# Routing sums of a two-layer transformer kernel, moved to four column tiles of the matrix engine

## What is computed

```
x = x + L0_xattn(layernorm(x), ctx)      # 8 heads
x = x + L0_ffn(layernorm(x))             # 16 experts of 64, the best 4 by sigmoid score
x = x + L1_xattn(layernorm(x), ctx)      # top-32 attention, FiLM, a long convolution, an MLP
x = x + L1_ffn(layernorm(x))             # 8 experts, each picks its best 512 tokens
```

```
logits = layernorm(x) @ expert_sel.T          # 16 per token
probs  = sigmoid(logits); take the best 4; divide by their sum
out    = sum over experts of  prob * relu(layernorm(x) @ keys[e]) @ values[e]
```

## Time and profile before

| what | value |
|---|---|
| median of three runs | 1471.42 us (1470.21 to 1471.47) |
| span of the profiled execution | 1470.0 us |
| TensorE busy | 1280.7 us, 87% |
| VectorE busy | 925.6 us, 63% |
| ScalarE busy | 465.3 us, 32% |
| GpSimd busy | 325.8 us, 22% |
| first routing matmul of the eight batches | 103.6, 240.0, 362.8, 485.4, 607.8, 739.4, 865.6, 974.8 us |

### The profile page before, as it was taken

The page is one execution under the profiler, slowest core; times in us unless marked ns, Lnnn a source line. Parts: engine busy times, 40 slices in busy tenths (PEclk is TensorE's granted clock), DMA queues, the critical chain, the costliest instruction groups (busy, mean ns, idle before and its releaser), DMA issues. The chain is left out here.

```text
span 1470.0 us, 17444 instructions
## 1 busy us (share of the span) xinstructions
PE 1280.7 (87%) x5222; PEld 768.4 (52%) x5222; DVE 925.6 (63%) x3439; ACT 465.3 (32%) x837; POOL 325.8 (22%) x598
## 2 busy tenths in 40 slices
PE   4677968999999899899989989999887719999996
PEld 3444644465466455546545554645444516666764
DVE  6647789767767776865677786686987382211110
ACT  2544432042324315213431521343132433233221
POOL 3121221023112203201220320222102303332331
PEclk9677989999999999989999999999998858999999
DMA  9002000200300400030030003003000025453321
GB/s 293 9 15 59 18 1 22 51 18 15 88 18 1 102 18 1 25 79 18 1 102 17 1 16 87 16 2 87 7 1 1 30 93 173 109 145 87 90 37 18
DMA packets 44904, 72.51 MB, mean 49 GB/s; under 512 B 8101, under 2 KB 26760, under 8 KB 44682
## 3 DMA queue, kind: packets, MB, share of 16 engines
q1 hardware_dynamic: 38666, 62.87, 14.6%
q0 software_dynamic: 6144, 8.52, 3.3%
HBM read 58.27 MB, written 13.07 MB: 49 GB/s over the span
## 5 line engine op out<-in xcount | busy, mean ns | idle before, releaser
L773 POOL TENSOR_SCALAR ve<-mv 128x2 f32<-128x2 f32 x74 | 16.6, 225 | 552.9 <-DVE mv L1041 552.8
L1604 PE MATMUL ps<-x,keys 128*128 128x512 f32 x256 | 127.0, 620 | 0.5 <-DVE hT L1133 0.4
L1761 PE MATMUL ps<-hT,values 128*128 128x512 f32 x256 | 118.2, 592 | 0.0
L2189 PE MATMUL experts_ps<-experts_yT,experts_fc 128*128 128x512 f32 x256 | 111.9, 595 | 1.2 <-ACT experts_yT L2114 1.2
L2201 PE MATMUL experts_ps<-experts_fc,experts_hT 128*128 128x256 f32 x512 | 112.0, 379 | 0.8 <-ACT experts_hT L2126 0.8
L1604 PE MATMUL ps<-zT_second,w 128*128 128x512 f32 x224 | 102.3, 598 | 7.8 <-ACT big L1552 7.2
L2201 PEld LDWEIGHTS experts_ps<-experts_fc,experts_hT 128*128 128x128 f32 x512 | 96.6, 190 | 14.6 <-ACT experts_hT L2126 1.6
L1604 PE MATMUL ps<-w,big 128*128 128x256 f32 x448 | 98.9, 380 | 0.8 <-ACT big L1552 0.8
L2098 DVE SCALAR_TENSOR_TENSOR experts_o<-experts_ps,experts_wh,experts_b2w 128x256 f32<-128x256 f32 x32 | 15.5, 484 | 128.7 <-PE experts_ps L2201 128.7
L2126 ACT ACTIVATE experts_hT<-experts_ps,experts_b 128x512 f32<-128x512 f32 x64 | 44.0, 687 | 155.4 <-PE experts_ps L2189 155.4
L1604 PEld LDWEIGHTS ps<-w,big 128*128 128x128 f32 x448 | 84.3, 190 | 13.8 <-ACT big L1552 1.6
(11 more groups left out here) (435 smaller groups left out, 2489.7 us busy)
## 6 DMA issues: line engine op xcount, KB each, us to landing
gT<-expert_gates SPq DMA_DIRECT2D x16, 1024.0 KB, 9.6
experts_fc<-in_fc1T SPq DMA_DIRECT2D x8, 1024.0 KB, 5.2
experts_fc<-in_fc2T SPq DMA_DIRECT2D x8, 1024.0 KB, 8.7
xT<-in_xT SPq DMA_DIRECT2D x8, 512.0 KB, 3.5
x<-in_x SPq DMA_DIRECT2D x8, 512.0 KB, 3.5
expert_table<-tb SPq DMA_DIRECT2D x7, 528.0 KB, 7.6
out_x<-x SPq DMA_DIRECT2D x7, 512.0 KB, 6.9
w<-in_W SPq DMA_DIRECT2D x2, 1024.0 KB, 9.4
```

The lines of the kernel that those rows point to most:

```text
L773: nc.gpsimd.tensor_scalar(o, i, c, None, ALU.add).then_inc(*tick(*event))
L1604: last = nc.tensor.matmul(o, l, r_, start=start, stop=stop)
L1761: last = nc.tensor.matmul(bank("O2", k), S["values"][:, c, k * P:(k + 1) * P], hT[:, c % RING, :], start=(c == 0), stop=(c == HC - 1))
L2189: last = nc.tensor.matmul(g_bank(m), fc1[e % 3][:, k, m * P:(m + 1) * P], yT[e % 2][:, k, :], start=(k == 0), stop=(k == DC - 1))
```

## The change

Both sums are computed by halves of the tokens (256 columns each) on four column tiles: scores and mean of the first half at PSUM partitions 0 to 16 and of the second at 32 to 48, the square sums of the halves at partitions 64 and 96. All lie in the first 256 columns of the bank. The column of 1/256 moves from the end of `sel` to its start, so that in each tile the sum that gives a mean stands at the tile's first partition.

One copy takes 97 partitions x 256 columns, now into a part of `e_buf` (`logits`) in place of `lists`. Partitions between the tiles hold what the bank held before; they are copied and not used. Two transposes (97 partitions x 128 tokens each) replace four. A transpose now holds the tokens of tile `g` of both halves, so token tile `t = 2h + g`, and VectorE's two readers take their elements in that order with patterns of one dimension more.

```diff
-            loads["sel"] = wb("sel", [P, DC, E0 + 1])[:, :, 0:E0], ...
+            loads["sel"] = wb("sel", [P, DC, E0 + 1])[:, :, 1:E0 + 1], ...
-            blank(g.memset(S["sel"][:, :, E0:E0 + 1], 1.0 / D))
+            blank(g.memset(S["sel"][:, :, 0:1], 1.0 / D))
 ...
                 for k in range(DC):
-                    nc.tensor.matmul(o[64:64 + E0 + 1, :], S["sel"][:, k, :], xp[:, k, :], start=(k == 0), stop=(k == DC - 1))
+                    for h in HALVES:
+                        nc.tensor.matmul(o[32 * h:32 * h + E0 + 1, 0:2 * P], S["sel"][:, k, :], xp[:, k, h * 2 * P:(h + 1) * 2 * P],
+                                         start=(k == 0), stop=(k == DC - 1))
                 pe.wait_ge(*at(b, "sq", DC - 1))
                 for k in range(DC):
-                    last = nc.tensor.matmul(o[96:97, :], S["sel"][:, k, E0:E0 + 1], sq[:, k, :], start=(k == 0), stop=(k == DC - 1))
+                    for h in HALVES:
+                        last = nc.tensor.matmul(o[64 + 32 * h:65 + 32 * h, 0:2 * P], S["sel"][:, k, 0:1], sq[:, k, h * 2 * P:(h + 1) * 2 * P],
+                                                start=(k == 0), stop=(k == DC - 1))
 ...
-                evacuate(b, lists[route_rows, :], bank("LG")[route_rows, :], "LG")
+                evacuate(b, logits, bank("LG")[routed, 0:2 * P], "LG")
 ...
-                for t in range(NT):
-                    last = nc.tensor.transpose(bank("LT")[:, t * 33:(t + 1) * 33], lists[route_rows, t * P:(t + 1) * P], ident[route_rows, route_rows])
+                for g in range(2):
+                    last = nc.tensor.transpose(bank("LT")[:, g * routed.stop:(g + 1) * routed.stop], logits[:, g * P:(g + 1) * P], ident[routed, routed])
 ...
-                    nc.vector.tensor_copy(ms[:], lg[:, :, E0:2 * E0 + 1:E0]).then_inc(*tick("ms"))
+                    nc.vector.tensor_copy(ms[:].rearrange("p (h g) k -> p g k h", g=2),
+                                          lg[:, :, 0:routed.stop:32].rearrange("p g (k h) -> p g k h", k=2)).then_inc(*tick("ms"))
 ...
-                    nc.vector.tensor_tensor(sg[:, :, 0:E0], lg[:, :, 0:E0], rr[:].to_broadcast([P, NT, E0]),
+                    nc.vector.tensor_tensor(sg[:].rearrange("p (h g) e -> p h g e", g=2)[:, :, :, 0:E0],
+                                            lg.rearrange("p g (h e) -> p h g e", h=2)[:, :, :, 1:E0 + 1],
+                                            rr[:].rearrange("p (h g) o -> p h g o", g=2).to_broadcast([P, 2, 2, E0]),
                                             ALU.mult).then_inc(*tick("emptied", "LT"))
```

More of the change, by code:

```diff
@@ L437, in layers_block @@
         sq = e_buf
+        logits = e_buf[0:3 * 32 + 1, 0, 0:2 * P]
         mx, sm, rs = (sb(n, [P, NT, H0]) for n in ("mx", "sm", "rs"))
@@ L443, in layers_block @@
         g16 = lists[32:32 + E0, :]
-        route_rows = slice(64, 64 + 33)
+        routed = slice(0, 3 * 32 + 1)
         ms, v0, ve0, rr = sb("route_ms", [P, NT, 2]), sb("route_var", [P, NT, 1]), sb("route_ve", [P, NT, 1]), sb("route_rstd", [P, NT, 1])
@@ L540, in layers_block @@
         half = [slice(0, 512), slice(512, HID)]
-        to_centre = [(S["sel"], slice(0, E0)), (S["keys"], half[0]), (S["keys"], half[1]), (S["gate_w"], slice(0, E1)),
+        to_centre = [(S["sel"], slice(1, E0 + 1)), (S["keys"], half[0]), (S["keys"], half[1]), (S["gate_w"], slice(0, E1)),
                      (S["w1"], half[0]), (S["w1"], half[1])]
@@ L1081, in gates @@
                 if part == 0:
-                    lg = bank("LT")[:, 0:NT * 33].rearrange("p (t e) -> p t e", t=NT)
+                    lg = bank("LT")[:, 0:2 * routed.stop].rearrange("p (g c) -> p g c", g=2)
                     v.wait_ge(*at(b, "filled", "LT"))
-                    nc.vector.tensor_copy(ms[:], lg[:, :, E0:2 * E0 + 1:E0]).then_inc(*tick("ms"))
+                    nc.vector.tensor_copy(ms[:].rearrange("p (h g) k -> p g k h", g=2),
+                                          lg[:, :, 0:routed.stop:32].rearrange("p g (k h) -> p g k h", k=2)).then_inc(*tick("ms"))
                     v.wait_ge(*at(b, "ms"))
@@ L1089, in gates @@
                 if part == 1:
-                    lg = bank("LT")[:, 0:NT * 33].rearrange("p (t e) -> p t e", t=NT)
+                    lg = bank("LT")[:, 0:2 * routed.stop].rearrange("p (g c) -> p g c", g=2)[:, :, 0:2 * 32]
                     v.wait_ge(*at(b, "rr"))
-                    nc.vector.tensor_tensor(sg[:, :, 0:E0], lg[:, :, 0:E0], rr[:].to_broadcast([P, NT, E0]),
+                    nc.vector.tensor_tensor(sg[:].rearrange("p (h g) e -> p h g e", g=2)[:, :, :, 0:E0],
+                                            lg.rearrange("p g (h e) -> p h g e", h=2)[:, :, :, 1:E0 + 1],
+                                            rr[:].rearrange("p (h g) o -> p h g o", g=2).to_broadcast([P, 2, 2, E0]),
                                             ALU.mult).then_inc(*tick("emptied", "LT"))
@@ L2234, in build @@
                 loads[name] = wb(name, [p, c, A[src].shape[1]])[:], A[src].rearrange("(c p) n -> p c n", p=p)
-            loads["sel"] = wb("sel", [P, DC, E0 + 1])[:, :, 0:E0], A["sel"].rearrange("(c p) n -> p c n", p=P)
+            loads["sel"] = wb("sel", [P, DC, E0 + 1])[:, :, 1:E0 + 1], A["sel"].rearrange("(c p) n -> p c n", p=P)
             loads["fd"] = wb("fd", [P, NT, 2 * P])[:], A["dft_in"].rearrange("(c p) f -> p c f", p=P)
```

## The result

The changed kernel takes 1477.61 us (median of four runs, 1475.79 to 1479.77) where the kernel before, beside it, takes 1471.04: the ratio is 1.0047, with a 95% interval of 1.0035 to 1.0059. It is 7 us slower, and 1467.9 was forecast. The profiled execution is the one of 1475.79 us; its span is 1474.0. Four of the runs further down had one execution each that was over 1.5% longer than the fastest of its kernel; their medians and the ratios leave it out.

A forecast was written before the change was run, and what follows sets the result against it. VectorE was taken as the bound for some 19 us after a routing, TensorE running ahead until it needs `am`. Gains of 0.8 + 1.59 + 1.1 = 3.5 us took 1471.42 to 1467.9; range 1462.5 to 1472.5.

The forecast's parts named there:

- The chain of one routing: Routing sums, copy and transposes: 0.86 + 0.21 + 0.07 = 1.14 us less per routing.
- Four tiles: Routing sums: four column tiles work at once, so the square sums take 0.86 us less.
- rivals B and C: B: tiles start in program order, 1469.2, chance 0.12; C: VectorE pays 0.34 us a batch for new order, 1470.7, 0.08.
- VectorE's 1.59 us in batches 2 to 5: VectorE's wait for the turned routing sums goes: 0.38 us each in batches 2 to 4, 0.44 in batch 5.
- TensorE's other 0.7 us a batch ends in the wait for `am`: Batches 2 to 5: TensorE's remaining saving is swallowed waiting for VectorE's attention weights, so it gains nothing.
- batch 1 at nothing: Batch 1: film matmul waits 2.03 us for a copy behind VectorE's gates; VectorE did not wait for sums; no gain.
- Rival D: The clock turns worse: one of batches 2, 3, 5, 6 falls into batch 4's pattern, costing 9.2 us; 1477, chance 0.10.
- batches 2 and 3 hold 0.99 with the same pieces: Argument against the clock turning worse: these stages keep granted clock 0.99 though made of the same pieces.
- Rival A: The clock turns better: batch 4 gets batch 3's pattern, 10.2 us gained in all, 1461.2 (in part 1464); chance 0.18.
- Batch 0 was to gain 0.8: Batch 0: between 0.4 and 1.14 us passes on, as TensorE's half-level stretch may halve a head start; 0.8 taken.
- Batch 6, entered at nothing: Batch 6: VectorE reads the sums without a wait and TensorE already waits 0.28 us for the gate; no gain.
- Batch 7 was to gain 1.1: Batch 7: VectorE waits 1.17 us for the sums and TensorE leads later, so its saving passes on: 1.1 us.

The follow-up runs named there:

- a_b1_fill1: Changed kernel with one extra 256-column matmul (result overwritten) in batch 1's wait for the copy of `am`; 1473.46 us, ratio 1.0025.
- b_again: The kernel before run once more, nothing altered; 1470.67 us, ratio 0.9997.
- a_held_fit: Changed kernel with three extra 256-column matmuls (1.29 us) behind the new transposes of batches 2 to 5; 1467.74 us.
- a_held_idle: Changed kernel with TensorE waiting for VectorE's variance, without extra work, behind the transposes of batches 2 to 5; 1471.25 us.
- a_again: The changed kernel run once more, nothing altered; 1477.54 us, ratio 1.0059.
- b_fill_am: Kernel before with three extra 512-column matmuls behind the first mlp product of batches 2 to 5; 1472.40 us, ratio 1.0016.
- a_fill_am: Changed kernel with three extra 512-column matmuls behind the first mlp product of batches 2 to 5; 1468.93 us, ratio 0.9996.
- b_shift: Kernel before with four extra 512-column matmuls once, in batch 0's mlp, delaying all that follows; 1473.30 us, ratio 1.0022.
- b_fill_fit: Kernel before with three extra 256-column matmuls behind the first mlp product of batches 2 to 5, four in batch 1's `am`-copy wait; 1474.84 us.
- a_fill_fit: Changed kernel with three extra 256-column matmuls in the `am` wait of batches 2 to 5, four in batch 1's `am`-copy wait; 1468.38 us.
- a_held_b1: Changed kernel with three extra 256-column matmuls behind the transposes of batches 2 to 5, one in batch 1's `am`-copy wait; 1467.23 us.
- b_half_sums: Kernel before with half of both routing sums left out (one of two channel halves); 1476.49 us, ratio 1.0023.
- a_fill_most: Changed kernel with extra 256-column matmuls in TensorE's waits for `am`, its batch 1 copy, expert scores, transform and gates; 1463.18 us.

## Why the prediction was wrong

**The chain of one routing: right.** 1.05 us less to the first transpose and 0.04 in the transposes (0.39 where 0.36 was taken), 1.09 against 1.14. The copy's median is 0.373 for 0.37. That partitions run side by side is in the trace of before: ScalarE's copies of 512 columns take a mean of 0.575 us with 16 partitions and 0.581 with 128.

**Four tiles: right, and rivals B and C fell.** In batch 7 the square sums start 0.03 us behind the row sums and the pairs follow each other every 0.21 to 0.22 us:

```profile
978.42 0.40 PE L1733 MATMUL ps<-x,sel 128*17 128x256 f32 x2
978.45 0.39 PE L1738 MATMUL ps<-e_buf,sel 128*1 128x256 f32 x2
978.65 0.39 PE L1733 MATMUL ps<-x,sel 128*17 128x256 f32 x2
...
978.86 0.39 PE L1733 MATMUL ps<-x,sel 128*17 128x256 f32 x2
```

All eight records of the row sums stand in the program ahead of the square sum that starts at 978.45, and six of them start behind it (pairs at 978.65, 978.86 and 979.08). So between column tiles this trace does not show starts in strict program order. VectorE's copy of the sums keeps its 0.16 us and its product with the root its 0.22.

**VectorE's 1.59 us in batches 2 to 5: right where the falls lie as before.** The waits are gone. What that is worth shows in a_b1_fill1, where two untouched stages have their falls within 1.3 us of where b_again has them: batch 2 takes 122.08 us against 122.58, batch 4 126.67 against 127.11, so 0.5 and 0.4 us less where 0.38 was taken. That a_held_fit is 3.4 us faster than the kernel before, against a forecast of 3.5, confirms no term: fillers and moved falls are in it as well.

**The step that failed** is "TensorE's other 0.7 us a batch ends in the wait for `am`", entered at nothing. The wait came (1.33 us in batch 3), but behind it the granted clock goes to 0.50 on film, second expert product and transform, which bound the stage, where before the fall had landed on a product that `am` covered. That cover stood in the trace of before (2.95 us for a product that takes 1.88 elsewhere) and I did not read it. It costs 3 to 4 us a stage. The same step entered batch 1 at nothing: 0.23 us more of a wait, 3.3 us more of a stage.

It also counts whether TensorE works while it is held: held behind the transposes by 1.29 us of work it gains 0.29% on the kernel before (a_held_fit, ratio 0.9971), and held there by a wait of 1.27 us nothing (a_held_idle, 1.0008), with a fall 4.4 us behind batch 3's routing that a_held_fit does not have. By what rule the clock falls and comes back, no run shows.

**Rival D named it, at a chance of 0.10.** Batches 2 and 3 did fall into batch 4's pattern: falls 15 and 25 us behind the routing, batch 4's 16 and 26. Against it stood "batches 2 and 3 hold 0.99 with the same pieces". The pieces were the same; their order against VectorE was not. Its price was off both ways: not one stage at 9.2 us but three at 3 to 4. That its 1477 is so near the measured 1477.6 is luck. That 9.2 came from batch 4's 131.6, which was one execution's: 127.1 and 124.0 in the other two with the old routing. Rival A's gain had the same root; batch 4's 3.6 us less in the profile is within that scatter.

**The rest.** Batch 0 was to gain 0.8: it is 0.8 us shorter in the first pair of profiles and 0.4 in the second (b_again, a_again), but b_fill_am, which has the old routing there, took 0.1 less than the changed kernel, so the term is not shown. Batch 6, entered at nothing, gained 0.95, and 0.90 in the second pair: both profiles of the kernel before have a fall 58 to 59 us behind that routing and both of the changed one have none; why was not followed up. Batch 7 was to gain 1.1: VectorE's wait went (0.11 us is left), but the stage to the end is 495.6 us where it was 495.2, with a half-level stretch from 1006.8 to 1010.3 us that the profile before does not have. In a_fill_am, which leaves batch 7 as it is in the changed kernel, that stretch is absent and the stage takes 493.93, 1.25 less than before. What brings the stretch was not tried; b_shift and b_fill_fit have it with the old routing.

**What stays open:** why fillers move falls on in batches 1 and 2 (a_fill_fit) rather than end them, and how the 10 us between the changed kernel and a_held_fit divide. Batches 1 to 3 are together 3.0 us shorter in a_held_fit's own profile than in the changed kernel's, and 9.4 in a_held_b1's. Other stages move too: from batch 7's routing to the end the profiles take from 493.9 to 499.5 us, though no filler stands there. In b_half_sums, whose profile is 4.8 us longer than that of before, that part is 4.35 longer, batches 2 and 3 are 7.7 longer, and batches 4 and 6 are 3.7 and 1.7 shorter. Why is not known.

## What to carry to other kernels

Time taken from TensorE ahead of a wait was not free here even where the wait swallowed it: 1.05 us less to the first transpose, 3.3 to 4.0 us more in each of three stages. Look at what TensorE does right behind the wait, and if that is bound work, price a stretch of it at a granted clock of 0.50; here it was 6.8 us long behind batch 3's wait, and the film product took 3.32 us in it where it takes 1.98 at 1.00. Where TensorE has to wait, put matmuls there that are needed anyway; here even useless ones paid (a_fill_most, 1463.18 us where the changed kernel takes 1477.61). And before a stage's length in one profile is used as a price, profile the same kernel again: one stage of the same kernel differed by up to 4.5 us between two profiles.

## What the runs showed of the hardware that was not expected

Four column tiles of one array ran beside each other (in batch 3 16 records of 0.38 us in 1.69 us, the wait for the squares included; in batch 7 16 of 0.39 us in 1.06 us, each tile starting one every 0.21 to 0.22 us, half of the 0.43 us that 512 columns take before), and started out of program order (six row-sum records behind a square sum that stands after them). A kernel that does strictly less (b_half_sums) was 0.2% slower, its stages of batches 2 and 3 at a granted clock of 0.96 where those of before had 0.99; one that does strictly more (a_fill_most) was 1% faster than the kernel it was made from. And executions of one kernel hold their half-level stretches in different stages: batch 3 of the kernel before took 122.4 us in one and 126.8 in another.
